# Two-layer transformer block on one core: in layer 0, TensorE's order within a slot, the order of ScalarE and VectorE, and the slot of the output product

## What is computed

```
xn = layernorm(x)
qkv = xn @ w_qkv.T                      # 32 query heads, 8 key/value heads, 64 wide
q, k = rope(rms_norm(q)), rope(rms_norm(k))
p = softmax(q k.T / 8), masked to the 64 keys up to the query
attn = (p v) @ w_out.T
ffn = (silu(xn @ Wg.T) * (xn @ Wu.T)) @ Wd.T      # 704 wide, weights from integers
x = x + attn + ffn
```

## Time and profile before

| what | us |
|---|---|
| median of 3 runs | 1113.39 |
| the three runs | 1099.7, 1113.72, 1113.39 |
| the profiled execution's own time | 1105.24 |
| its span, from the first instruction to the last | 1103.5 |
| granted clock, mean over the span | 0.944 |

### The profile page before, as it was taken

One profiled execution on the slowest core, in us unless ns is written; L12 is line 12 of the kernel. 1 busy time (PEld: TensorE's weight loads), 2 busy tenths in 40 slices (PEclk: granted clock), 3 DMA queues, 4 the chain that ended last, 5 costly groups with the idle time before them and its releaser, 6 DMA issues. The chain is left out here.

```text
span 1103.5 us, 26418 instructions
## 1 busy us (share of the span) xinstructions
PE 963.0 (87%) x8729; PEld 507.3 (46%) x8729; DVE 833.2 (76%) x1762; ACT 689.4 (62%) x1791; POOL 703.0 (64%) x1003
## 2 busy tenths in 40 slices
PE   3688898898898898899889886478999999999997
PEld 2355565555555555556556553343222222333324
DVE  6798777787777787778777774257999999888941
ACT  2555665565555555556555552015999999888992
POOL 4677888887787887887897883322555565332221
PEclk9889999999999999999999998568999999999999
DMA  5746554544444434434454433511111211311001
GB/s 194 160 70 129 101 92 86 87 86 89 84 83 94 84 78 93 92 77 94 91 81 89 85 84 55 189 39 20 21 37 25 33 28 22 50 30 35 7 2 39
DMA packets 241675, 81.00 MB, mean 73 GB/s; under 512 B 215876, under 2 KB 240132, under 8 KB 241284
## 3 DMA queue, kind: packets, MB, share of 16 engines
q1 hardware_dynamic: 239044, 74.85, 34.0%
q10 hardware_dynamic: 2496, 4.46, 1.2%
HBM read 18.49 MB, written 4.19 MB: 21 GB/s over the span
## 5 line engine op out<-in xcount | busy, mean ns | idle before, releaser
L1253 DVE TENSOR_REDUCE l_mxv<-l_mx 128x1 f32<-128x1024 f32 x256 | 295.0, 1217 | 33.0 <-PE l_mx L1439 31.8
L1164 ACT ACTIVATE l_prob<-l_sc 128x512 f32<-128x512 f32 x512 | 273.0, 605 | 23.6 <-PE l_sc L1447 22.4
L704 POOL TENSOR_TENSOR t<-t 128x320 f32<-128x320 f32 x128 | 114.0, 890 | 114.8 <-DVE t L581 114.4
L1439 PE MATMUL l_mx<-l_kt,l_qt 48*128 48x512 f16 x512 | 155.7, 386 | 15.8 <-DVE l_mxv L1253 13.7
L1447 PE MATMUL l_sc<-l_qt,l_kt 50*128 50x512 f16 x512 | 156.0, 382 | 0.8 <-ACT l_prob L1164 0.8
L695 POOL TENSOR_TENSOR rm<-ss,half_neg 128x5 f32<-128x5 f32 x128 | 156.0, 1219 | 0.0
L1418 PE MATMUL l_acc<-l_prob,qkv_all 128*17 128x256 f32 x2048 | 153.9, 384 | 0.0
L837 PE MATMUL pv<-v,probs 128*64 128x65 f32 x2048 | 90.4, 230 | 63.7 <-ACT probs L480 33.3
L386 ACT ACTIVATE nat<-t 128x128 f16<-128x128 f32 (+1 forms) x256 | 78.8, 358 | 98.8 <-POOL t L721 98.6
L480 ACT ACTIVATE probs<-sc,neg_bound 128x512 f32<-128x512 f32 x128 | 87.1, 681 | 68.9 <-PE sc L878 68.8
L1307 POOL TENSOR_SCALAR l_mxs<-l_mxv 128x8 f32<-128x8 f32 x32 | 7.5, 235 | 186.3 <-DVE l_mxv L1253 186.3
(11 more groups left out here) (177 smaller groups left out, 2151.4 us busy)
## 6 DMA issues: line engine op xcount, KB each, us to landing
qkv_all<-w_qkv SPq DMA_DIRECT2D x3, 768.0 KB, 8.1
v<-v SPq DMA_DIRECT2D x64, 32.5 KB, 1.9
xn_all<-xs SPq DMA_DIRECT2D x16, 128.5 KB, 2.3
xa<-x SPq DMA_DIRECT2D x16, 128.0 KB, 2.4
tk<-nat SPq DMA_TRANSPOSE x128, 2.7
qkv_all<-w_o SPq DMA_DIRECT2D x8, 256.0 KB, 3.9
ats<-an SPq DMA_TRANSPOSE x128, 2.3
xc<-x SPq DMA_DIRECT2D x16, 128.0 KB, 2.3
```

The lines of the kernel that those rows point to most:

```text
L704: pool.tensor_tensor(t1[:, b, :, :], t1[:, b, :, :], t2[:, :, :], ALU.add).then_inc(s_["pool_u"], 1)
L1164: act.activation(prob[:, (y * NI + u) % NPR, h * 512:(h + 1) * 512], sc[:, k % NSC, :], ACT.Exp, scale=D1 ** -0.5).then_inc(s_["act_sc"], 1)
L1253: dve.tensor_reduce(mxv[:, x % 2, u:u + 1], mx[:, MX[k] % 2, :], AX.X, ALU.max).then_inc(s_["dve_mx"], 1)
L1439: ins = pe.matmul(mx[:, MX[kx] % 2, keys], qt[r:r + KS, tile % 4, u * P:(u + 1) * P], kt[r:r + KS, tile % 4, keys], start=True, stop=True)
```

## The change

The stage lags change, and with them where each stage stands: the output product's two lags go down by one (LAG_O 9 to 8, LAG_W 10 to 9), and ScalarE's and VectorE's part of a feed-forward chunk gets a lag of its own, LAG_H = 5, a slot after TensorE's. WD_K becomes 2. The steps that follow a tile's last output product (x1, norms, stores, ranking) all move one slot sooner.

The scores' six matmuls now all use 128 rows: the masks' upper 64 rows are set to zero once, and the semaphore between the two parts is gone. SyncE's order of stages is as before; the stores of a finished tile are a slot sooner. The core of the diff:

```diff
+LAG_H = 5
-LAG_O = 9
-LAG_W = 10
-WD_K = 1
+LAG_O = 8
+LAG_W = 9
+WD_K = 2
...
 def way(n):
-    return (n + 3) * G if n >= NT - 2 else (n + 3) * G + 4
+    return (n + 2) * G + 7 if n >= NT - 2 else (n + 3) * G + 4
...
 @block.scalar, in each slot
-                n, k, ok = at(s, LAG_O)
-                if ok:
-                    m = n * G + k
-                    act.wait_ge(s_["dve_an"], m + 1)
-                    if m >= 2:
-                        act.wait_ge(at_ld[m % NA], 16 * (m // NA))
-                    ev(an16[:, m % 2, 0, :, :], an[:, m % 2, :, :]).then_inc(s_["act_an"], 1)
+                c = (s - LAG_H) % 16 // 2
+                i = (s - LAG_H) // 16
+                if s >= LAG_H and s % 2 == LAG_H % 2 and c < NF and i < NI:
...
+                    act.activation(th[0:m, :, :], ff[0:m, 0, :, :], ACT.Tanh, scale=sgp[0:m, c:c + 1]
...
 (sq, v1 and xh as before)
+                n, k, ok = at(s, LAG_O)
+                if ok:
...
+                    ev(an16[:, m % 2, 0, :, :], an[:, m % 2, :, :]).then_inc(s_["act_an"], 1)
+                n, k, ok = at(s, LAG_S)
+                b = k % 2
+                if ok:
+                    act.wait_ge(s_["pe_S"], n * G + k + 1)
+                    wait(act, s_["pe_V"], n * G + k - 1)
+                    act.activation(pm[:, b, :, :, :], sc[:, :, 0:REP * WIN]...
 (nat, rest, kc and kt as before; th and the exponential behind them are gone)
...
 @block.vector
+            dve.memset(mk[0:HD, :, :], 0.0)
...
 @block.tensor
-                    pe.matmul(weights[0], keys(n, k, 1, 0, top), queries(n, k, 0, top), start=True, stop=False)
-                    pe.matmul(weights[1], outside(n, 1), eyes, start=True, stop=False)
-                    pe.matmul(weights[0], keys(n, k, 0, 0, full), queries(n, k, 0, full), start=False, stop=False)
-                    pe.matmul(weights[1], keys(n, k, 0, 1, full), queries(n, k, 1, full), start=False, stop=False
-                              ).then_inc(s_["pe_S1"], 1)
+                    for h in range(2):
+                        pe.matmul(weights[h], keys(n, k, 0, h), queries(n, k, h), start=True, stop=False)
+                        pe.matmul(weights[h], keys(n, k, 1, h), queries(n, k, h), start=False, stop=False)
+                        ins = pe.matmul(weights[h], outside(n, h), eyes, start=False, stop=True)
+                    ins.then_inc(s_["pe_S"], 1)
...
-                    pe.wait_ge(s_["pe_S1"], n * G + k + 1)
-                    pe.matmul(weights[0], outside(n, 0), eyes, start=False, stop=True)
-                    pe.matmul(weights[1], keys(n, k, 1, 1, top), queries(n, k, 1, top), start=False, stop=True
-                              ).then_inc(s_["pe_S"], 1)
```

More of the change, by code:

```diff
@@ L558, in _ @@
                                              ).then_inc(s_["dve_x1"], 1)
[L559 to L565, removed]
+                c = (s - LAG_H) % 16 // 2
+                i = (s - LAG_H) // 16
+                if s >= LAG_H and s % 2 == LAG_H % 2 and c < NF and i < NI:
+                    m = chunk(c)[1]
+                    dve.wait_ge(s_["act_th"], i * NF + c + 1)
+                    wait(dve, s_["dve_h"], i * NF + c)
+                    wait(dve, s_["dve_wr"], min(NT, (s - 3) // G - 1 - ((s - 3) % G == 0)))
+                    dve.scalar_tensor_tensor(fa[0:m, :, :], th[0:m, :, :], 1.0, ff[0:m, 0, :, :], ALU.add,
+                                             ALU.mult).then_inc(s_["dve_a"], 1)
+                    dve.wait_ge(s_["dve_a"], i * NF + c + 1)
+                    if i >= 1:
+                        dve.wait_ge(s_["pe_W"], (i * B - 1) * G + WD_K + c + 1)
+                    dve.scalar_tensor_tensor(ht[0:m, c, :, :], ff[0:m, 1, :, :], sgu[0:m, c:c + 1], fa[0:m, :, :], ALU.mult,
+                                             ALU.mult).then_inc(s_["dve_h"], 1)
                 n, k, ok = at(s, LAG_A)
@@ L782, in _, with keys, queries @@
             pe.wait_ge(eye_ld, 16)
-            full, top, low = slice(0, P), slice(0, HD), slice(HD, P)
-            eyes = idh[low, HD:P].unsqueeze(1).broadcast_to([HD, REP, WIN])
+            eyes = idh[:, HD:P].unsqueeze(1).broadcast_to([P, REP, WIN])
             weights = [sc[:, h, 0:REP * WIN].rearrange("p (r q) -> p r q", r=REP) for h in range(2)]
[L788 to L792, removed]
+            def keys(n, k, j, h):
+                return tk[:, (n * G + k) % NQ, j, h * WIN:h * WIN + P]
+            def queries(n, k, h):
+                return tk[:, (n * G + k) % NQ, 2:NB, (h + 1) * WIN:(h + 2) * WIN]
             def outside(n, h):
-                return mk[low, 0 if n < B and h == 0 else 1, :]
+                return mk[:, 0 if n < B and h == 0 else 1, :]
             for s in TIMES:
@@ L811, in _ @@
                     ins.then_inc(s_["pe_A"], 1)
[L812 to L819, removed]
-                    wait(pe, s_["dve_h"], i * NF + f)
-                    for u in range(2):
-                        for c in range(KC):
-                            for j, (a, w) in enumerate(((xh, gu_hi), (xh, gu_lo), (xl, gu_hi))):
-                                ins = pe.matmul(ff[0:m, u, :, :], w[:, u, c, cols], a[:, i % 2, c, :, :],
-                                                start=(c == 0 and j == 0), stop=(c == KC - 1 and j == 2))
-                    ins.then_inc(s_["pe_F"], 1)
                 n, k, ok = at(s, LAG_V)
@@ L848, in _ @@
                         pe.wait_ge(s_["set_k"], 1)
[L849 to L853 removed]
+                    for h in range(2):
[3 more added lines that the diff above has]
+                    ins.then_inc(s_["pe_S"], 1)
+                f = (s - LAG_F0) % 16 // 2
+                i = (s - LAG_F0) // 16
+                if s >= LAG_F0 and s % 2 == LAG_F0 % 2 and f < NF and i < NI:
+                    cols, m = chunk(f)
+                    pe.wait_ge(s_["dve_xl"], i * B + 2)
+                    if i == 0:
+                        pe.wait_ge(s_["dve_gu"], f + 1)
+                    wait(pe, s_["dve_h"], i * NF + f)
+                    for u in range(2):
+                        for c in range(KC):
+                            for j, (a, w) in enumerate(((xh, gu_hi), (xh, gu_lo), (xl, gu_hi))):
+                                ins = pe.matmul(ff[0:m, u, :, :], w[:, u, c, cols], a[:, i % 2, c, :, :],
+                                                start=(c == 0 and j == 0), stop=(c == KC - 1 and j == 2))
+                    ins.then_inc(s_["pe_F"], 1)
                 n, k, ok = at(s, LAG_W)
```

91 lines of the change are left out of this document (38 added, 53 removed).

## The result

| | before | after |
|---|---|---|
| median, us | 1110.22 (the three runs and one more) | 1202.52 (1191.7 to 1214.92, 4 runs) |
| ratio to before | | 1.081 (95%: 1.075 to 1.088) |
| profiled execution's span | 1103.5 | 1200.7 |
| layer 1's first instruction on GpSimd, from the start | 699.61 | 783.30 |
| the rest of the span (layer 1) | 403.9 | 417.4 |

What follows compares the result with a forecast made beforehand. TensorE was nearest the bound before; after, ScalarE's serial wait for VectorE was to set a 4.93 us floor, plus 0.30 for lumps: 5.23 against 5.00, x 128 = +29.4 on 1105, giving 1135 us, range 1096 to 1169.

Steps and rivals of the forecast that it cites:

- What bounds the kernel before: Layer 0's slots: TensorE, busy 4.53 of 5.00 us, is nearest the bound; values product waits 0.46 per slot.
- TensorE's matmuls: Scores on TensorE: whole matmuls cost nothing over half-array pairs; 0.10 us per slot goes, 13 us if TensorE sets the time.
- The chain in series: ScalarE waits each slot for VectorE's trip from v1 to an, 2.01 us, making a slot at least 4.93 us.
- The stand: ScalarE's idle time ahead of an16, waiting for VectorE's an: 2.01 us in each slot.
- VectorE's lumps: VectorE's other work behind nat low exceeds its free time by 0.30 us per slot, making a slot 5.23 us.
- the sum: Layer 0's 128 slots at 5.23 instead of 5.00 us: +29.4 us, giving 1135.
- floor: Shortest possible slot, ScalarE's own work plus its wait for an and the feed-forward extra: 4.93 us.
- The clock: TensorE, idle 0.7 us or more per slot, might be granted less clock than 0.96; part of the worse case.
- The output product a slot sooner: The output product's wait for its transpose ats stays hidden, with 0.5 us of cover; nothing in the total.
- Faster: Rival, chance 0.09: TensorE's backlog sets the pace, not the round trip; slot 4.43 to 4.53 us, 1032 to 1045 us.
- Hidden lumps: Rival, chance 0.28: VectorE's lumps overlap ScalarE's extra layer 1 steps; slot 4.93 to 5.15 us, 1096 to 1124 us.
- Worse than forecast: Inside the forecast's case (0.62): lower TensorE clock or late transpose; 5.5 us per slot, +64 us, 1169.

Runs made afterwards that it cites:

- e2: The kernel before with the six score matmuls whole (128 rows) and together where the first four stood: 1093.35 us, ratio 0.985.
- e10: The changed kernel with one spare VectorE sum per slot right behind ss, ahead of an: 1247.08 us, ratio 1.125.
- e8: The changed kernel with only VectorE's reciprocal and an moved ahead of t1, t2 and ss: 1111.96 us, ratio 1.000.
- e11: The changed kernel with one spare VectorE sum per slot behind nat low: 1204.43 us, ratio 1.085.
- e1: The changed kernel with ScalarE's three copies for layer 1 (xt and two into its store) moved ahead of an16: 1143.23 us, ratio 1.032.
- e5: e1 with the output product and the steps behind it back in their old slots, and a third buffer for ats: 1131.36 us, ratio 1.017.
- e7: e6 with the output product back in its old slot and a third buffer for ats, as in e5: 1081.62 us, ratio 0.974.
- e6: e1 with VectorE's reciprocal and an moved ahead of t1, t2 and ss: 1105.58 us, ratio 0.994.
- e3: e2 plus the new orders on TensorE, ScalarE and VectorE, with an16 and the output product in their old slots: 1089.85 us, ratio 0.984.
- e9: e3 with reciprocal and an ahead of t1, and layer 1's copies ahead of the exponential: 1095.62 us, ratio 0.987.

## Why the prediction was right and wrong

- **What bounds the kernel before.** TensorE near full, waiting for exponential and an. The wait for an went (20.8 to 0), the one for the exponential hardly changed (25.1 to 23.4), and the time went the other way. The reading that the exponential is late because ScalarE does it last was half of it: in the earlier trace rows it waits 56.5 us itself, for the scores.
- **TensorE's matmuls.** "Making them full costs nothing" held, and 0.10 x 128 = 13 us less "if TensorE sets the time" was right in kind: e2 gives 16. The reading of the Trainium skill (TensorEngine Tiling (Array Packing), "Key Properties") by which the pair runs in the time of one would have made it 28 us more; e2 speaks against that. It does not speak against the drain that the same place names, and what the 0.21 us of a pair consists of was not separated.
- **The chain in series.** Right, in place and in size. The stand was 2.01 in the working; in the trace it is 2.00 in many slots, 1.73 where xh stands in it, up to 3.6, and 2.22 on the mean; a plain slot by the same rows is 2.74 from an16 to t1 and 1.88 on to the next an16, 4.62, and is 4.53 to 4.54. Three runs show it as a cause: e10 (lengthen it), e8 (shorten it), e11 (the same work beside it). A slot under 4.5 us, which the working ruled out, does not occur in 100 to 600 us: the shortest is 4.53.
- **VectorE's lumps.** 5.23 us per slot; e1, the kernel without layer 1's waits, has 5.21. That kernel is 33 us slower than before (1143.2 against 1109.8), 30.7 in layer 0, where the sum had 29.4. Some of this agreement is luck, since two errors cancel in it: e5, with the product back in its slot, is 12 us lower (16 in layer 0), and the sum had nothing for the product. So floor and lumps together were counted too high, by some 8 us by the medians and 15 by layer 0's time.
- **The step that failed** is in the sum, by what it leaves out: "All else of VectorE's is done in lumps behind nat low" counted the extra work of VectorE and the length of ScalarE's, but no wait of TensorE for ScalarE: that term stood at nothing. Layer 1's products wait in TensorE's queue, ahead of the next projection, for copies that ScalarE's list has behind the exponential and nat. Before, they did not wait (0.0 idle, L903 above), so the trace of before had no row that warned of it. The working asked what is queued behind an16 on ScalarE, and did not go on to ask which engine waits for those later entries. Its size is 59 us (e1), 53 of them in layer 0 (783.3 against 730.3), and nearly all of it lies in two slots of each tile, that with the copy xt and the one behind it. In the four of those slots in which the four products run in 1.98 us the excess over e1 is 2.0 to 2.8 us, near the 1.5 to 2.5 us that TensorE stands for xt in them; the larger excesses, to 5.5 us, have slower products in them. The sign that the prediction gave, exponentials 5.2 to 5.3 us apart, was missed by the changed kernel (5.62) and met by e1 (5.21).
- **The clock** stood in the forecast as "granted less clock than the 0.96". The mean did not fall in layer 0's steady part, but in some slots with the copy xt it fell. Set the products at 248.74 above beside these:

```profile
476.50 3.78 PE L898 MATMUL extra<-win,xt 128*128 128x512 f32 x4 [1.08 <-ACT xt L387]
480.07 0.53 PE L810 MATMUL qk<-wq_hi,xh 128*128 128x384 f16 x1
480.39 0.53 PE L810 MATMUL qk<-wq_lo,xh 128*128 128x384 f16 x1
```

The four products take 3.78 instead of 1.98, and projections start 0.32 apart instead of 0.16: TensorE is at the lower of its two levels, 1.2 GHz and not 2.4 (granted clock 0.50 from 476.5 to 482.3, 1.00 from 248.7 to 251.7). All of that is on the loop, since ScalarE waits for this projection:

```profile
482.24 0.44 ACT L407 ACTIVATE sq<-qk 128x320 f32<-128x320 f32 x1 [5.19 <-PE qk L810]
```

- **The output product a slot sooner** was to be hidden with 0.5 us to spare. e5 puts it at 12 us, and at 24 where the stand is short (e7 against e6). The median of 2.3 was the wrong number to set against so small a cover, the longest being 4.4; and in 21 of 38 waits the cover was not there even at 2.3.
- **The rivals.** "Faster", with a decision point of about 1.6 us for ScalarE's stand, was decided by the 2.00. "Hidden lumps" (4.93 to 5.15 us, 1096 to 1124) is not out: e1's slot is 5.21, but e5, without the product's wait, has 98 an16 in 500 us, 5.10, and layer 0 is 14.7 us longer than before, inside that rival's -9 to +19. How much of the lumps is hidden stays open. "Worse than forecast" had a price of 64 us and the wrong mechanisms for most of it.

What stays open: the 13.5 us of layer 1. In the thirteen profiled executions, none with a changed instruction there, its part of the span goes from 403.9 to 422.2 us. Before, at 0.95, has the shortest part and the highest mean clock; the other twelve have 408.1 to 422.2 at 0.89 to 0.92. So before is the odd one, and nothing ties the difference to this change. Open too is what holds e3 and e9 at 1090 to 1096.

## What to carry to other kernels

When engines work in slots, write down for each engine's list the trips that go out to another engine and come back within the slot: their length is added to that engine's work, and an engine that was busy 57% of the time (ScalarE in rows 1) can then set the pace. Then follow every engine that waits for a later entry of that list, since it inherits the stand; e8 shows that both nearly go if the two instructions that the trip is for come first. And an added 0.5 us of idle work at a suspected place, against the same work a little later, tells in one pair of runs whether the place is on the loop. Compare the slots one by one: the whole times (45 and 2 us) had up to 8 us of layer 1's scatter in them.

## What the runs showed of the hardware that was not expected

A pair of matmuls on the two halves of the rows starts at the same time, but the two took 0.21 us to the next start, as much as two of all 128 rows; for the first pair of the scores (L849 and L850) it is 0.21 or 0.22 in 94 of the 100 slots. The kernel with whole ones, which also has all six together, was 16 us faster (e2). The clock did not follow the idle time directly ahead: after 1.95 us of standing the products at 248.74 ran at the full level, after 1.08 us those at 476.50 at the lower. More had gone before the second: TensorE had also stood 2.08 us for ats up to 474.16, and was busy 2.76 of the 6.5 us from 470.0, against 2.80 of the 4.7 us from 244.0 ahead of the first. And layer 1, untouched, took 403.9 us before and 417.4 after, at a mean granted clock of 0.95 and 0.90.
